# A fused attention and feed-forward kernel on one core: the division cut into three calls, one wait moved, and all five engines' calls in a new order

## The reference

```python
u = norm(x)
x_norm = layer_norm(u, ln1_w, ln1_b)
Q = elu(x_norm @ q_w.T + q_b) + 1 ; K = elu(x_norm @ k_w.T + k_b) + 1 ; V = x_norm @ v_w.T + v_b
# causal linear attention: num_t = sum_{s<=t} (Q_t.K_s) V_s ; den_t = sum_{s<=t} Q_t.K_s + 1e-6
x1 = u + (num / den) @ o_w.T + o_b
x2 = x1 + gelu(layer_norm(x1, ln2_w, ln2_b) @ f1_w.T + f1_b) @ f2_w.T + f2_b
x  = x + x2
h  = gelu(norm(x) @ absmean(W_fc).T)               # absmean: weights made -1, 0 or 1
out = x + layer_norm(h, ln_w, ln_b) @ absmean(W_proj).T
```

## Time and profile before

| | us |
|---|---|
| median of 3 runs | 453.47 (453.27 to 454.2) |
| the profiled execution | 453.58 |
| its span, first to last instruction | 451.9 |
| PE busy | 436.9 |
| DVE busy | 360.3 |
| ACT busy | 310.0 |
| POOL busy | 238.0 |

### The profile page before, as it was taken

One profiled execution on the slowest core, in us unless ns is written; L12 is line 12 of the kernel. 1 busy time (PEld: TensorE's weight loads), 2 busy tenths in 40 slices (PEclk: granted clock), 3 DMA queues, 4 the chain that ended last, 5 costly groups with the idle time before them and its releaser, 6 DMA issues.

```text
span 451.9 us, 8867 instructions
## 1 busy us (share of the span) xinstructions
PE 436.9 (97%) x2942; PEld 392.8 (87%) x2942; DVE 360.3 (80%) x1200; ACT 310.0 (69%) x580; POOL 238.0 (53%) x224
## 2 busy tenths in 40 slices
PE   4899999999999999999999999999999999999997
PEld 3697898899988999889989999888988899888976
DVE  6899998787688779787799589996599937985595
ACT  4888858984377855979367864888379745775263
POOL 3894266834565229673766068961755044435135
PEclk9999999999999999999999999999999999999999
DMA  7223200202011003021002103102001000000011
GB/s 249 113 95 141 66 30 0 66 31 47 1 47 48 1 5 138 20 75 48 2 1 94 46 2 95 43 7 93 1 1 48 25 2 0 25 1 1 1 47 49
DMA packets 13518, 20.41 MB, mean 45 GB/s; under 512 B 2720, under 2 KB 11040, under 8 KB 12960
## 3 DMA queue, kind: packets, MB, share of 16 engines
q1 hardware_dynamic: 13472, 19.84, 13.5%
HBM read 15.62 MB, written 4.22 MB: 44 GB/s over the span
## 4 chain that ended last, share of the span: by engine, by line
PE 76%; DVE 12%; ACT 4%; issue 3%; DMA 2%; POOL 2%; SPq 1%; POOLq 0%; ACTq 0%; DVEq 0%
PE bank_f L490 10%; PE bank_p L538 9%; PE bank_y L264 6%; PE bank_y L265 6%; PE bank_y L263 6%; PE bank_f L263 6%; PE bank_f L265 6%; PE bank_f L264 6%; PE bank_y L504 5%; PE bank_a L263 3%; PE bank_a L264 3%; PE bank_a L265 3%; DMA h<-in_f 2%; DVE g_lo L1167 2%; DVE bn L1153 2%
## 5 line engine op out<-in xcount | busy, mean ns | idle before, releaser
L1337 POOL TENSOR_TENSOR rs<-ve,neg_half 128x2 f32<-128x2 f32 x48 | 33.5, 700 | 81.9 <-DVE ve L969 79.4
L263 PE MATMUL bank_y<-wf_hi,h_hi 128*128 128x256 f32 x240 | 67.1, 279 | 0.0
L264 PE MATMUL bank_y<-wf_lo,h_hi 128*128 128x256 f32 x240 | 67.1, 279 | 0.0
L265 PE MATMUL bank_y<-wf_hi,h_lo 128*128 128x256 f32 x240 | 67.0, 279 | 0.0
L761 ACT ACTIVATE bank_f<-bank_f,f_bias 128x512 f32<-128x512 f32 x64 | 42.3, 662 | 27.4 <-PE bank_f L265 26.4
L538 PE MATMUL bank_p<-wpj_t,g_hi 128*128 128x256 f32 x240 | 60.2, 288 | 0.0
L1167 DVE SCALAR_TENSOR_TENSOR g_lo<-bank_y,vec,g_hi 128x256 fp32r<-128x256 f32 x128 | 54.7, 477 | 6.1 <-ACT g_hi L798 5.5
L1032 DVE TENSOR_TENSOR h_lo<-bank_f,h_hi 128x512 fp32r<-128x512 f32 x60 | 40.8, 687 | 23.2 <-ACT h_hi L769 22.7
L798 ACT ACTIVATE g_hi<-bank_y,vec 128x256 fp32r<-128x256 f32 x128 | 52.4, 478 | 9.1 <-PE bank_y L504 6.2
L538 PE MATMUL bank_p<-wpj_t,g_lo 128*128 128x256 f32 x240 | 58.1, 279 | 0.0
L789 ACT ACTIVATE h<-bank_f 128x512 f32<-128x512 f32 x64 | 37.8, 600 | 24.7 <-PE bank_f L490 24.2
(11 more groups left out here) (298 smaller groups left out, 1212.3 us busy)
## 6 DMA issues: line engine op xcount, KB each, us to landing
out<-y_yc SPq DMA_DIRECT2D x15, 256.0 KB, 2.5
lines_b<-lines SPq DMA_DIRECT2D x6, 512.0 KB, 4.2
u<-in_xt SPq DMA_DIRECT2D x6, 512.0 KB, 4.8
x_even<-in_x SPq DMA_DIRECT2D x8, 256.0 KB, 2.9
x_odd<-in_x SPq DMA_DIRECT2D x8, 256.0 KB, 3.0
h<-in_f SPq DMA_DIRECT2D x1, 1024.0 KB, 8.2
y_yc<-in_f SPq DMA_DIRECT2D x1, 1024.0 KB, 10.6
h<-in_fc SPq DMA_DIRECT2D x1, 1024.0 KB, 4.9
```

The lines of the kernel that those rows point to most:

```text
L263: pe.matmul(ps, w[0], r[0], start=start, stop=False, skip_group_check=skip)
L264: pe.matmul(ps, w[0], r[1], start=False, stop=False, skip_group_check=skip)
L265: return pe.matmul(ps, w[1], r[0], start=False, stop=stop, skip_group_check=skip)
L1337: pool.tensor_tensor(rs[n][:, 2 * h:2 * h + 2], ve[n][:, 2 * h:2 * h + 2], neg_half[:, 0:2], ALU.pow).then_inc(s[f"ln{n + 1}_rs"], 1)
```

## The change

It does three things.

1. `attn_out` becomes three calls, `attn_den`, `attn_rec` and `attn_out`, each with its own wait. The instructions are the same.
2. The wait for the fourth norm's aggregated statistics leaves `aggregate` and goes to the head of `ln4_var`. The instructions are the same.
3. Every `order()`, and the list of DMAs on SP, is written anew. No other call is added or taken away: PE has 437 calls before and after, ACT 432, POOL 165, DVE 546 before and 610 after (64 more by the split). The matmuls, the transposes, the DMAs and their sizes are the same.

```diff
@@ aggregate
                     dve.bn_aggr(mv[n][:, t, :], bn[n][:, t, :]).then_inc(s[f"ln{n + 1}_mv"], 1)
-                dve.wait_ge(s[f"ln{n + 1}_mv"], mv_count)
+                if n < 3:
+                    dve.wait_ge(s[f"ln{n + 1}_mv"], mv_count)
@@
-            def attn_out(g, t):
-
-                b = a_bank(g, (2, 0, 1, 2)[t])
+            def attn_den(g, t):
                 dve.wait_ge(s["av_done"], 4 * g + t + 1)
-                dve.tensor_scalar(den[:, t:t + 1], b[:, D:D + 1], 1.0, ATTN_EPS, ALU.mult, ALU.add).then_inc(s["den_ready"], 1)
+                dve.tensor_scalar(den[:, t:t + 1], a_bank(g, (2, 0, 1, 2)[t])[:, D:D + 1], 1.0, ATTN_EPS,
+                                  ALU.mult, ALU.add).then_inc(s["den_ready"], 1)
+
+            def attn_rec(g, t):
                 dve.wait_ge(s["den_ready"], 4 * g + t + 1)
                 dve.reciprocal(rden[:, t:t + 1], den[:, t:t + 1]).then_inc(s["rden_ready"], 1)
+
+            def attn_out(g, t):
                 dve.wait_ge(s["rden_ready"], 4 * g + t + 1)
                 dve.wait_ge(s["n1o_ready"], 2 * g + t // 2 + 1)
@@
             def ln4_var(g, h):
+                dve.wait_ge(s["ln4_mv"], 4 * g + 2 * h + 2)
                 variance(3, g, h)
@@ TensorE, order(): the opening, and around the third norm of group 1
-                qkb(); tu(0, 0); tu(0, 1); wvo_mm(); qk_mm(0); bvo(); fill(); scores(0); v_mm(0, 0); v_mm(0, 1)
+                qkb(); wvo_mm(); tu(0, 0); tu(0, 1); bvo(); qk_mm(0); fill(); v_mm(0, 0); scores(0); v_mm(0, 1)
...
-                f1(1, 7); attend(2, 0); f2(1, 4); f2(1, 5); f2(1, 6); f2(1, 7); proj(0, 1, 1); attend(2, 1)
-                attend(2, 2); attend(2, 3); proj(0, 1, 2); tz3(1, 0); tz3(1, 1); proj(0, 1, 3); fc(1, 0, 0)
+                f1(1, 7); f2(1, 4); f2(1, 5); f2(1, 6); f2(1, 7); v_mm(2, 1); attend(2, 0); attend(2, 1)
+                proj(0, 1, 1); proj(0, 1, 2); proj(0, 1, 3); attend(2, 2); tz3(1, 0); tz3(1, 1); attend(2, 3)
@@ GpSimd, order(): the opening
-                consts(); ln1_rstd(0, 0); ln1_rstd(0, 1); n1_rstd(0); wf1_lo(0); ln1_rstd(1, 0); wf1_lo(1); wf1_lo(2)
+                n1_rstd(0); ln1_rstd(0, 0); ln1_rstd(0, 1); consts(); wf1_lo(0); wf1_lo(1); wf1_lo(2); wf1_lo(3)
@@ VectorE, order(): the opening, and the third norm of the last group
-                consts(); ln1_stats(0, 0); ln1_stats(0, 1); dcol(); ln1_shift(0, 0); u_odd(0, 0); ln1_shift(0, 1)
-                u_odd(0, 1); qk_bias_add(); n1_ve(0); u_lo(0, 0); wqk_lo(); u_lo(0, 1); wide_cols(); n1_shift(0)
+                consts(); ln1_stats(0, 0); ln1_stats(0, 1); n1_ve(0); dcol(); wide_cols(); n1_shift(0); qk_bias_add()
+                wqk_lo(); ln1_shift(0, 0); ln1_shift(0, 1); u_odd(0, 0); u_odd(0, 1); u_lo(0, 0); u_lo(0, 1)
...
-                h_lo(7, 5); h_lo(7, 6); g_lo(6, 1, 3); h_lo(7, 7); y_sum(7, 0); ln4_shift(6, 1); ln3_stats(7, 0)
-                ln3_shift(7, 0); z3_odd(7, 0); z3_lo(7, 0); y_sum(7, 1); ln3_stats(7, 1); ln4_stats(7, 0)
-                ln3_shift(7, 1); z3_odd(7, 1); ln4_stats(7, 1); ln4_var(7, 0); z3_lo(7, 1); g_lo(7, 0, 0)
+                y_sum(7, 0); ln3_stats(7, 0); ln3_shift(7, 0); z3_odd(7, 0); z3_lo(7, 0); y_sum(7, 1); ln3_stats(7, 1)
+                ln3_shift(7, 1); z3_odd(7, 1); ln4_shift(6, 1); ln4_stats(7, 0); ln4_stats(7, 1); z3_lo(7, 1)
@@ TensorE, order(): the last group
-                proj(6, 1, 1); f2h(7, 3, 1); f2h(7, 4, 1); tz3(7, 0); f2h(7, 5, 1); f2h(7, 6, 1); f2h(7, 7, 1)
-                fc(7, 0, 0); fc(7, 0, 1); fc(7, 1, 0); fc(7, 1, 1); tr(7, 0, 0); tr(7, 0, 1); tz3(7, 1); proj(6, 1, 2)
-                proj(6, 1, 3); fc(7, 2, 0); fc(7, 2, 1); fc(7, 3, 0); fc(7, 3, 1); tr(7, 0, 2); tr(7, 0, 3)
+                f2h(7, 4, 1); f2h(7, 5, 1); tz3(7, 0); f2h(7, 6, 1); f2h(7, 7, 1); proj(6, 1, 1); fc(7, 0, 0)
+                fc(7, 0, 1); fc(7, 1, 0); fc(7, 1, 1); proj(6, 1, 2); tz3(7, 1); tr(7, 0, 0); proj(6, 1, 3)
+                tr(7, 0, 1); fc(7, 2, 0); fc(7, 2, 1); fc(7, 3, 0); fc(7, 3, 1); tr(7, 0, 2); proj(7, 0, 0)
@@ ScalarE, order(): around group 6's third and fourth fc tiles
-                g_hi(6, 0, 0); z2_norm(7, 0); gelu3(6, 2, 0); gelu3(6, 2, 1); g_hi(6, 0, 1); z2_norm(7, 1)
-                g_hi(6, 0, 2); z2_hi(7, 0); z2_hi(7, 1); gelu3(6, 3, 0); gelu3(6, 3, 1); g_hi(6, 0, 3); g_hi(6, 1, 0)
+                gelu3(6, 0, 1); gelu3(6, 1, 0); gelu3(6, 1, 1); g_hi(6, 0, 0); z2_norm(7, 0); z2_norm(7, 1)
+                z2_hi(7, 0); g_hi(6, 0, 1); g_hi(6, 0, 2); z2_hi(7, 1); gelu3(6, 2, 0); gelu3(6, 2, 1); gelu3(6, 3, 0)
```

426 lines of the change are left out of this document (219 added, 207 removed).

## The result

| | us |
|---|---|
| before, median of 20 runs | 453.59 (453.15 to 454.79) |
| after, median of 20 runs | 454.64 (453.44 to 455.77) |
| ratio, 95% interval | 1.0018, 1.0011 to 1.0026 |
| profiled execution of after | 455.77, span 454.0 |
| the same kernel once more, median of 11 | 454.44 |

The forecast was 451.2 us, with a range up to 454.3. The ratio is an estimate over all rounds; that of the two medians is 1.0023, inside the interval. The first profile of after fell on the slowest of its 20 runs; the second, 1.3 us shorter, lies at the median, and where a single stop is sized I use both.

The account below looks back on a forecast made before the run. The prediction took PE's list of matmuls, plus PE's waits, to bound the kernel. Its terms, 0 - 1.7 + 0.5 - 0.25 - 0.9 = -2.35 us, took 453.58 to 451.2 us, range 449.3 to 454.3.

Parts of the forecast that it names:

- The opening: PE's list up to 60 us: scores(0) at 20.2, small gains and losses cancel, sum 0; bounds 0.8 gained, 1.5 lost.
- 1.5 lost if every 0.3 to 0.5 of these adds up: Lower bound up to 60 us: the small delays, such as f1(0, 0) 0.3 and f1(0, 2) 0.4 us later, all add up.
- The middle: 60 to 420 us: 0.9 us at group 1's third norm and 0.8 of small waits go, gain 1.7; new waits counted separately.
- the three smaller waits: PE waits of 0.25 to 0.3 us between 60 and 420 us, one before scores(6); expected to go, 0.8 us together.
- The transposes: Each run of transposes costs the next matmul 0.08 us; 60 runs instead of 63, so -0.25 us.
- The end: Last tz3 and after: z3_odd(7, 1) no longer beside POOL's addition, tz3(7, 1) doesn't wait; -0.9 us, bounds -1.3 and 0.
- 0.5 us of new waits: Group 6: more ACT calls ahead of gelu3(6, 2, 0), waits before tz2(7, 1) and fc(6, 3, 0); +0.5, bounds 0 and 2.
- The split: Division in three calls returns at most 7.7 us to DVE's queue, which has 90 us idle; costed at nothing for PE.
- a gain ends at the waits that end on a late queue: Upper bound on the gain from the divided division and moved wait: 1.2 + 0.8 us of PE's waits up to 420 us.
- the first: Rival: the waits only move and the middle gains nothing; -0.65 us, 452.8, chance 0.16.
- the second: Rival: divisions ahead of third- and fourth-norm work cost six middle groups 0.5 us each; +0.65 us, 454.3, chance 0.13.
- The third: Rival: a shorter DVE queue returns the 7.7 us and small waits vanish everywhere; about -4.3 us, 449.3, chance 0.13.

Follow-up runs that it names:

- the best kernel: Before with the end of after and the division in three calls, eight adjacent pairs of attn_out interleaved: 452.04 us, ratio 0.9968 to before.

## Why the prediction was wrong, point by point

**The opening, 0 forecast, +1.4 measured.** Two terms were mis-sized. The first is `wvo_mm` "2.27 us long", "so PE has done both by about 11.2": it took 3.55 us, the transposes behind it 1.69, and both were done at 12.80. That moved `qk_mm(0)` to 14.47 instead of 12.9, and `scores(0)` to 21.28 instead of 20.2, outside the 19.8 to 20.8 that was named, though not past 21.5. At `attend(0, 0)` the two profiles are 0.5 us behind that of before. The price was read from a trace in which PE reached its full pace within `wvo_mm`, and in both profiles of after it did so 2.2 us later. That was chance as much as order: in three other kernels with this opening the full pace came at 10.6 to 10.8 us, and there `scores(0)` started at 20.39 to 20.45, where the prediction had it. The second is `f1(0, 0)` "0.3 us later": the durations were those of before, and the step read the collision of the earlier trace rows as a thing of the end. A pair of this kind met at 33 us, where I had not looked for which POOL instruction would be running. That is 1.1 us, and the run with `wf2_lo(3)` later shows 1.04 of them. What the range allowed, "1.5 lost if every 0.3 to 0.5 of these adds up", was right in size by luck: the loss came by other causes.

**The middle, -1.7 forecast, +0.7 measured, or +1.2 with the third stage of group 0.** The 0.9 us at group 1's third norm came as forecast. The 0.8 us of the three smaller waits did not: they went, and three of 0.3 to 0.4 us came (ahead of `proj(0, 1, 0)`, `f2(4, 0)` and, in some profiles, `tz3(4, 1)`), beside the 0.5 at `fc(0, 1, 0)`. The step that failed is the count of "the PE work that lies between the call that starts the chain and the call that needs its end". It sizes the cover, and takes the chain's own length from before; but that length depends on what stands ahead on ACT and DVE, and there four `g_lo` in a row, or `u_hi(2, 0)` ahead of `gelu3(0, 0, 0)`, made it longer. The rest of the middle's loss lies in single starts that are 0.05 to 0.18 us late; `f2` calls and what follows them show six of these (before: one of 0.09 and the 0.28 of the earlier trace rows). Read beside VectorE's list they are short waits of the same kind. In the second profile `f2(2, 4)` starts at 157.20, 0.06 behind the end of `h_lo(2, 4)`, ahead of which VectorE had stood 1.17 us for ScalarE's high part of K; and `scores(6)` starts at 321.53, 0.05 behind the end of `qk_lo(6)`: the wait of the earlier trace rows, 0.18 us long instead of 0.28. Where the rest of the 0.7 us lies stays open.

**The transposes, -0.25.** Too small to be seen under this.

**The end, -0.9 forecast, -1.1 by itself.** The mechanism was right, and one call carries it; its size was 0.2 short, since the stop of 0.35 us ahead of `fc(7, 2, 0)` did not come. The table's -1.6 begins at `fc(6, 0, 0)`: the other 0.5 come from group 6's third stage, ahead of `f1(7, 0)` and in the `f1` stretch, just where the prediction had put 0.5 us of new waits (its `gelu3(6, 2, 0)` behind five other ACT calls). With that term's place in the end, the middle proper stands at -1.7 forecast and +0.7 measured.

**The split, 0 forecast, about -1.3 in the new order and -0.4 in the old, the latter not clear of the noise.** The bound "a gain ends at the waits that end on a late queue" was right; what was wrong was to take those waits as already counted. In the new order DVE's queue is late at more places than the old trace shows; with the divisions joined, the trace has 0.8 us more lateness in the middle and 0.4 more at the end. Only one of these places is visible by name, so that this is how the 1.3 us arise is in part argued. Read against the sentence of the Trainium skill's page "VectorE: DVE Perf Modes" that a semaphore between operations costs nothing, the measurement decides for the starts of the earlier trace rows, in these operations of one column.

**The rivals.** None as it was written. The waits moved, as the first had it, but with losses beside; the second put its price on divisions in front of norms, and joining them made the kernel slower, so as a net price it is refuted. Even `ln2_var(0, 1)`, which comes 0.5 us later behind `attend(0, 0)` than in before (6.21 us against 5.73), is not late by the pairs: with the divisions joined it comes at 6.76. What stands ahead of it in the new list are the two `ln1_shift` of group 1, 0.24 us each. The third's mechanism, a shorter queue, is real and was more than paid for elsewhere.

**Checks of the profile.** Held: no gap before `tz3(1, ...)`, `z3_odd(7, 1)` at 0.41, DVE and PE within 2 us. At the edge: PE's stops of over 0.2 us after 60 us, which add up to 2.0 us in the second profile (0.51, 0.32, 0.36, 0.32, 0.48), and to about 2.7 in the first. Missed: `scores(0)`. The two signs of failure that were named, `scores(0)` after 21.5 and waits of 0.3 us in each middle group, did not come, and the prediction failed all the same: neither looked at what `f1(0, 0)` waits for.

## What to carry to other kernels

When lists are reordered, the durations of the old trace don't carry over for VectorE and GpSimd operations on SBUF: lay the two lists side by side in time and look for new meetings, above all ahead of a norm that TensorE waits for; one small call moved off such a meeting was worth 1.1 us of the 1.5 that the best kernel gained. An order of five engines is one object: of the nine runs here that set a piece of one order into the other, five lost over 3 us by a wait that neither whole order has, and in three of the five TensorE's granted clock read 0.50 behind the wait, which added 1.4 to 1.5 us to it. And the cover in front of a call says nothing until the chain under it is worked out through the new queues of every engine on it.

## What the runs showed of the hardware

**The pace of TensorE at the start.** The eight matmuls of `wvo_mm` start 0.43 us apart or 0.22, and a transpose takes 0.21 us to the next or 0.11. In each trace all of PE's rows go at the slow pace up to one moment and at the fast one behind it: 10.6 us in before, within `wvo_mm`; 12.8 in both profiles of after, behind the transposes. At this same moment the trace's list of clock records begins (10.61, 12.79 and 12.77), with 1.00. Ahead of its first record the column of the granted clock reads 1.00 as well, but nothing was recorded there. The slow pace is the one that PE has where the record says 0.50: in the run with `wf2_lo(3)` later, 512 columns take 0.43 us at 0.50 and 0.23 at 1.00. So I read the start as the 1.2 GHz level; that is inferred from the pace, not recorded.

When the fast pace comes is not set by the order. PE's first row lies at 6.4 to 7.0 us everywhere; the change comes at 10.6 to 13.3 us in the nine profiles with the old opening and at 10.6 to 13.4 in the ten with the new one (16.3 with the transposes first, where PE stood 2.68 us). In the old opening `wvo_mm` took 2.3 us in the profile of before, 2.5 and 2.6 in two others and 3.06 in six, so the 2.27 of the earlier trace rows was the best of its kind, and a term that rested on it was up to 0.8 us short even without the change. What the moment costs depends on the opening: in the new one `attend(0, 0)` starts at 24.07 to 24.14 us in the three profiles with a change by 10.8 us and at 24.62 to 25.07 in the seven others; in the old one it starts at 23.78 to 24.78, without such a relation.

**The clock behind a long stop.** Stops of 1.93, 2.98, 3.04 and 4.34 us (the new opening ahead of the old rest; the old order up to the end; TensorE's whole order at group 1's third norm; `wf2_lo(3)` later) were each followed or ended by a granted clock of 0.50 for 3.4 to 6.8 us. Stops of 1.08, 1.35, 1.53, 1.87 and 1.92 us were not. So such a stop can cost well over its length: 1.93 us of waiting went with some 1.5 us of slow matmuls.

**A semaphore just in time.** It isn't free for PE. `f2(3, 7)` of the second profile starts where it should, 0.05 us behind the end of its `h_lo`, but its second matmul starts 0.22 us behind the first instead of 0.12, and no idle time stands in the rows:

```profile
218.77 0.39 PE L263 MATMUL bank_y<-wf_hi,h_hi 128*128 128x256 f32 x1
218.99 0.28 PE L264 MATMUL bank_y<-wf_lo,h_hi 128*128 128x256 f32 x1
```

The six such starts of the new order's `f2` calls come to 0.7 us together.
